# A fused LayerNorm, attention and gated-MLP kernel: the first stage's instructions, weight loads and buffer fills in another order

## The chip, the cores and the metric

One Trainium2 chip. The batch has eight sequences, and each of the eight cores runs the same program on one of them (2048 rows of 1024 numbers); the cores exchange nothing. The time is the device time of the slowest core in microseconds, median over runs.

## The reference

For each sequence `x` (float32, 2048 x 1024), with 16 heads of 64 and a hidden width of 3072:

```python
xn = (x - mean(x)) / sqrt(var(x) + 1e-5)
q, k, v = split(xn @ W_attn + b_attn)
att = q @ k.T / 8 / temperature + slope[h] * (j - i), masked to j <= i
y = (softmax(att) @ v) @ W_proj + b_proj
f = (silu(xn @ Wg.T) * (xn @ Wu.T)) @ Wd.T      # int weights / 127
out = x + y + f
```

## The kernel before, in words

The five engines run in-order programs written by hand, tied together by semaphores; nothing is scheduled by a compiler. There are three stages.

**First stage.** The sequence is cut into 16 tiles of 128 rows. For tile i: SyncE loads it (`xstage`, four buffers; load i waits for `v_xn` >= i-3, that is for tile i-4 to be normalised). VectorE takes statistics (two `bn_stats` L503, one `bn_aggr` L506). ScalarE takes the root of the variance (L641). VectorE takes its reciprocal (L510) and writes the normalised tile as bf16 (`xn_st`, L514). TensorE transposes it in eight matmuls with the identity (L745) into `ps_s` or `ps_gu` in turn, and ScalarE copies it into `xnT` (L648). `xnT` holds the whole sequence and is read by everything that follows. From it TensorE makes the values: a *value unit* is one row tile by one half (8 heads), eight matmuls of 512 columns into one of the two halves of `ps_t` (L770), copied to `Vt` by ScalarE (L656). The weights `wv_b` are loaded as two halves by GpSimd, whose DMAs also cast float32 to bf16 (L413). For each 512 rows, TensorE also makes q and k of the first pair of heads (*q/k unit*, two times eight matmuls, L710); VectorE copies q out (`evac_q`, L481), ScalarE copies k out (`evac_k`, L616). One matmul of one column (L752) turns the temperature into a vector, read back at L644.

The order before is one loop over tiles on each engine. TensorE's iteration i transposes tile i and then makes the values of tile i-1. ScalarE's iteration i takes the root of tile i, copies out transpose i-2 and then the values of that round. VectorE takes the statistics of tile i and then normalises tile i-1:

```python
for i in range(NT + 1):          # VectorE
    if i < NT: ...               # bn_stats x2, bn_aggr of tile i
    if i: ...                    # reciprocal, tensor_scalar of tile i-1
```

GpSimd, once x tiles 0 and 1 have landed, issues `wv_b` half 0, `wqk_b` of pair 0, `wv_b` half 1, and then fills rows 64 to 103 of `qx` and `kx` with twelve bf16 memsets (L421 to L425). Once tile 11 is normalised it issues the first two pairs of gate and up weights (`cast_gu(0)`, `cast_gu(1)`, L405 and L406), `wqk_b` of pair 1 and the output projection `wpj_b` (2 MB in bf16, L430).

**Second stage** (from L801 on in TensorE's program). `attention_plan` lists steps; each has score matmuls (L821), key-side matmuls (L802), value products (L837) and 512-column gate/up matmuls (L730) mixed in. `silu(f)` is GpSimd's part of gate/up unit f; its later weight loads are issued between those. **Third stage:** output projection plus down projection (L884, L889).

TensorE enters the second stage only behind the last q/k unit, when the last `evac_q`, `evac_k` and value copies are done. SyncE issues the shifts of q and k into `qx` and `kx` (L322) behind all its x loads.

## Time and profile before

| | |
|---|---|
| median of 3 runs | 1144.08 us (1143.51 to 1230.53) |
| the profiled execution | 1145.15 us |
| its span, first to last instruction of the slowest core (core 2) | 1143.6 us |
| spans of the eight cores | 1138.9 to 1143.6 us |
| TensorE matmul busy | 1084.3 us, 95% |
| VectorE, ScalarE, GpSimd busy | 628.9, 479.4, 267.1 us |

Times in the profile are counted from the span's start. An engine's idle time before an instruction is given with what ended it. A matmul's end is modelled, so rates are read from start to start.

### The profile page before, as it was taken

The numbers are of one execution on the slowest core, as the hardware profiler recorded it, in microseconds if no ns is written. First come the engines' busy times: TensorE is split into PE (matmuls) and PEld (weight loads), VectorE is DVE, ScalarE is ACT, GpSimd is POOL, SyncE is SP. The second block draws the span as 40 slices with busy tenths as digits, with TensorE's granted clock in tenths as the row PEclk, the third lists the DMA queues.
The fourth block names the chain that finished last, engine by engine and source line by source line (L and its number), as shares of the span: only waits on it lengthen the run. The fifth ranks groups of instructions, "written<-read, shape, count | busy, mean of one in ns | idle before, by whom it ended". The sixth has DMA issues, their size and how long they took to land.

```text
span 1143.6 us, 23885 instructions; the slowest of 8 cores (1138.9 to 1143.6 us)
## 1 busy us (share of the span) xinstructions
PE 1084.3 (95%) x7366; PEld 551.8 (48%) x7510; DVE 628.9 (55%) x1254; ACT 479.4 (42%) x869; POOL 267.1 (23%) x289
## 2 busy tenths in 40 slices
PE   3899899999999999999999999999999999999998
PEld 1344355555555545555555555555555344444443
DVE  5541867777776777677777777677873100000100
ACT  1443345655555555565565556555656200000000
POOL 7210121322222222132222112112223422222220
PEclk9999999999999999999999999999999999999999
DMA  8439023433413332153321213113521652525222
GB/s 185 132 93 176 19 53 75 79 71 71 89 34 66 78 83 63 42 88 67 68 59 34 62 42 62 34 31 73 168 61 38 217 189 74 184 74 184 74 74 74
DMA packets 57069, 98.34 MB, mean 86 GB/s; under 512 B 23292, under 2 KB 43909, under 8 KB 55862
## 3 DMA queue, kind: packets, MB, share of 16 engines
q0 software_dynamic: 7872, 35.66, 16.3%
q1 hardware_dynamic: 46178, 52.65, 15.6%
q10 hardware_dynamic: 2900, 8.51, 1.9%
q8 instruction: 68, 1.11, 0.4%
q14 instruction: 51, 0.42, 0.1%
HBM read 90.50 MB, written 27.26 MB: 103 GB/s over the span
## 4 chain that ended last, share of the span: by engine, by line
PE 86%; DVE 6%; issue 4%; DMA 2%; ACT 1%; POOL 1%; DVEq 0%; ACTq 0%; POOLq 0%; SPq 0%
PE ps_gu L730 24%; PE ps_dn L889 14%; PE ps_s L821 11%; PE ps_t L802 9%; PE ps_m L710 9%; PE ps_y L837 5%; PE ps_dn L884 5%; PE ps_t L770 5%; DVE cm L555 3%; DMA xstage<-xin 1%; PE ps_s L824 1%; PE ps_t L806 1%; DMA tile_s<-tiles 1%; DVE hst L491 1%; DVE nm L575 0%
## 5 line engine op out<-in xcount | busy, mean ns | idle before, releaser
L555 DVE TENSOR_REDUCE cm<-ps_s 128x1 f32<-128x512 f32 (+3 forms) x640 | 378.1, 607 | 144.6 <-PE ps_s L821 81.3
L672 ACT ACTIVATE pt<-ps_t 128x512 bf16<-128x512 f32 (+1 forms) x576 | 328.7, 575 | 297.8 <-PE ps_t L802 191.1
L730 PE MATMUL ps_gu<-xnT,wubuf 128*128 128x512 bf16 x720 | 246.1, 378 | 3.3 <-DVE hst L491 2.3
L730 PE MATMUL ps_gu<-xnT,wgbuf 128*128 128x512 bf16 x714 | 244.7, 378 | 2.4 <-ACT kst L616 1.2
L821 PE MATMUL ps_s<-kx,qx 67*128 67x512 bf16 (+3 forms) x640 | 213.7, 347 | 16.7 <-DVE cm L555 11.6
L802 PE MATMUL ps_t<-qx,kx 104*128 104x512 bf16 (+3 forms) x640 | 216.3, 348 | 1.5 <-DVE qx L585 0.8
L433 POOL TENSOR_SCALAR th_s<-th_s 128x512 f32<-128x512 f32 x96 | 59.4, 618 | 615.7 <-ACT th_s L624 615.7
L889 PE MATMUL ps_dn<-wdres,hb 128*128 128x512 bf16 x753 | 167.7, 379 | 0.8
L837 PEld LDWEIGHTS ps_y<-Vt,pt 128*128 128x128 bf16 x2176 | 125.3, 97 | 81.7 <-issue 0.2
L837 PE MATMUL ps_y<-Vt,pt 128*128 128x65 bf16 x2176 | 138.8, 193 | 0.5
L605 DVE SCALAR_TENSOR_TENSOR outsb<-ps_dn,xres 128x512 f32<-128x512 f32 x32 | 20.7, 686 | 205.1 <-PE ps_dn L889 205.1
L710 PE MATMUL ps_m<-xnT,wqk_b 128*128 128x512 bf16 x466 | 120.0, 378 | 0.7
L889 PEld LDWEIGHTS ps_dn<-wdres,hb 128*128 128x128 bf16 x768 | 75.1, 98 | 90.6
L439 POOL TENSOR_TENSOR gs_s<-th_s,gh_s 128x512 bf16<-128x512 f32 x96 | 111.0, 1156 | 26.4 <-POOL th_s L433 26.4
L821 PEld LDWEIGHTS ps_s<-kx,qx 67*128 67x128 bf16 x640 | 61.7, 96 | 102.9 <-issue 52.3
L730 PEld LDWEIGHTS ps_gu<-xnT,wubuf 128*128 128x128 bf16 x768 | 73.0, 98 | 57.0 <-issue 5.9
L730 PEld LDWEIGHTS ps_gu<-xnT,wgbuf 128*128 128x128 bf16 x768 | 73.5, 98 | 51.9 <-issue 1.9
L491 DVE SCALAR_TENSOR_TENSOR hst<-ps_gu,gs_s 128x512 bf16<-128x512 f32 x96 | 65.9, 686 | 39.3 <-POOL gs_s L439 32.5
L802 PEld LDWEIGHTS ps_t<-qx,kx 104*128 104x128 bf16 x640 | 63.3, 99 | 30.0 <-issue 4.0
L624 ACT ACTIVATE th_s<-ps_gu 128x512 f32<-128x512 f32 x96 | 57.1, 594 | 32.3 <-PE ps_gu L730 31.7
L770 PE MATMUL ps_t<-wv_b,xnT 128*128 128x512 bf16 x250 | 62.3, 403 | 4.7 <-DMA wv_b<-wv_r 2.7
L710 PEld LDWEIGHTS ps_m<-xnT,wqk_b 128*128 128x128 bf16 x480 | 41.9, 97 | 39.8 <-issue 0.4
(74 smaller groups left out, 737.1 us busy)
## 6 DMA issues: line engine op xcount, KB each, us to landing
h_sc<-hst SPq DMA_DIRECT2D x96, 128.0 KB, 1.9
hb<-h_sc SPq DMA_DIRECT2D x4, 3072.0 KB, 13.8
xstage<-xin SPq DMA_DIRECT2D x16, 512.0 KB, 6.8
xres<-xin POOLq DMA_DIRECT2D x16, 512.0 KB, 4.7
out<-outsb ACTq DMA_DIRECT2D x15, 512.0 KB, 2.7
wgbuf<-wg_r POOLq DMA_DIRECT2D x12, 512.0 KB, 5.7
wubuf<-wu_r POOLq DMA_DIRECT2D x12, 512.0 KB, 8.8
wd_sc<-wd_r POOLq DMA_DIRECT2D x12, 512.0 KB, 7.8
```

The lines of the kernel that those rows point to most:

```text
L433: e.tensor_scalar(th_s[f % 2][:, :], th_s[f % 2][:, :], 1.0, 1.0, AluOpType.add, AluOpType.mult).then_inc(sem["g_th"], 1)
L439: e.tensor_tensor(gs_s[f % 2][:, :], th_s[f % 2][:, :], gh_s[f % 2][:, :], AluOpType.mult).then_inc(sem["g_s"], 1)
L491: e.scalar_tensor_tensor(hst[f % 4][:, :], ps_gu[:, 512:1024], 1.0 / 127.0, gs_s[f % 2][:, :], AluOpType.mult, AluOpType.mult).then_inc(se ...
L555: e.tensor_reduce(cm[:, c0:c0 + 1], ps_s[:, s % 2 * 512:s % 2 * 512 + w], AX.X, AluOpType.max, negate=True).then_inc(sem["v_mx"], 1)
L672: e.activation(pt[t % NPT][:, 0:w], ps_t[:, t % 2 * 512:t % 2 * 512 + w], AF.Exp).then_inc(sem["a_e"], 1)
L710: mm = e.matmul(ps[:, :], wqk_b[p % 2][:, f0 + dc * 256:f0 + dc * 256 + 128], xnT[:, dc * T + tc * 512:dc * T + (tc + 1) * 512], start=(dc ...
L730: mm = e.matmul(ps_gu[:, r // 8 * 512:r // 8 * 512 + 512], w[:, w0:w0 + 128], xnT[:, dc * T + tb * 512:dc * T + tb * 512 + 512], start=(dc ...
L770: mm = e.matmul(ps_t[:, n % 2 * 512:n % 2 * 512 + 512], xnT[:, dc * T + tt * 128:dc * T + (tt + 1) * 128], wv_b[:, half * 4096 + dc * 512: ...
L802: mm = e.matmul(ps_t[:, c0 + off:c0 + off + w], k_[0:KT, kt * 128:(kt + 1) * 128], q_[0:KT, b * 512 + i0 * 128:(b + 1) * 512], start=(x == ...
L821: mm = e.matmul(ps_s[:, r0:r0 + w], q_[0:KS, b * 512 + i * 128:b * 512 + (i + 1) * 128], k_[0:KS, c0:c0 + w], start=True, stop=not diag)
L837: mm = e.matmul(ps_y[:, i * VW:(i + 1) * VW], pt[a % NPT][:, c0:c0 + 128], Vt[:, (kt * H + h) * VW:(kt * H + h + 1) * VW], start=(T0[n] == ...
L889: return e.matmul(ps_dn[:, r0:r0 + 512], hb[tb % 2][:, hc * 512 + ts * 128:hc * 512 + ts * 128 + 128], wdres[:, hc * 1024 + half * 512:hc ...
```

## The change

No arithmetic is changed except how constants are written into `qx` and `kx` (as 32-bit words, so half as many elements per fill). Everything else is order:

- VectorE: the code is split into `statistics(i)` and `normalise(i)`. Statistics of tiles 0 and 1 come first, then both are normalised; tile 2 as one; from tile 3 on `statistics(i + 1)` stands ahead of `normalise(i)`. `evac_q` 0, 1, 2 stand behind tiles 6, 8 and 13 (before: in iterations 6, 10 and 14).
- ScalarE: a first root on `eps_s` right at the start; then an order written out by hand: roots (`deviation`) of tiles 0 and 1, transposes 0 and 1, and so on. For tiles 4 to 7 the root stands behind the copy of the transpose before it. From tile 8 on, roots are three tiles and transposes two tiles ahead of the values of `for i`.
- TensorE: transposes 0 and 1, value units 0 and 1, transposes 2 and 3, then per tile 4 to 7 one value unit and one transpose; all values of tiles 0 to 7 in half 0 come before any of half 1; the second q/k unit before the first unit of half 1; then transposes two tiles ahead.
- GpSimd: `wv_b` half 0 in two pieces, issued when x tile 0 and x tile 1 have landed; `wqk_b` when the second piece has landed; half 1 when `wqk_b` has landed; six fills then, the other six behind tile 12; `cast_gu(1)` behind `silu(0)`, `wpj_b` behind `silu(6)`.
- SyncE: the load of x tile 3 waits for the first piece of `wv_b`.

```diff
 # SyncE
             for i in range(NT):
+                if i == 3:
+                    e.wait_ge(sem["l_wva"], 16)
...
 # GpSimd
+            e.dma_start(out=wv_b[:, 0:2048], in_=wv_r[0, :, 0:2048]).then_inc(sem["l_wva"], 16)
             e.wait_ge(sem["l_x1"], 16)
...
+            e.dma_start(out=wv_b[:, 2048:4096], in_=wv_r[0, :, 2048:4096]).then_inc(sem["l_wvb"], 16)
+            e.wait_ge(sem["l_wvb"], 16)
+            cast_qk(0)
+            e.wait_ge(sem["l_wq0"], 16)
+            e.dma_start(out=wv_b[:, 4096:6144], in_=wv_r[1, :, 0:2048]).then_inc(sem["l_wv1"], 16)
+            e.dma_start(out=wv_b[:, 6144:8192], in_=wv_r[1, :, 2048:4096]).then_inc(sem["l_wv1"], 16)
+            set_rows(0, 1)
             e.wait_ge(sem["v_xn"], NT - 4)
             cast_gu(0)
-            cast_gu(1)
             cast_qk(1)
-            e.dma_start(out=wpj_b[:, :], in_=wproj_r[:, :]).then_inc(sem["l_wp"], 16)
+            set_rows(1, 7)
...
             for f in range(NF):
                 silu(f)
+                if f == 0:
+                    cast_gu(1)
+                if f == 6:
+                    e.dma_start(out=wpj_b[:, :], in_=wproj_r[:, :]).then_inc(sem["l_wp"], 16)
...
 # VectorE
+            for i in range(3, NT):
+                if i + 1 < NT:
+                    statistics(i + 1)
+                normalise(i)
...
 # ScalarE
+            for i in range(4, 8):
+                deviation(i)
+                evac_v(i - 2, i - 1)
+                if i == 6:
+                    evac_k(0, 0)
+                evac_x(i)
...
+            for i in range(8, NT):
+                if i + 3 < NT:
+                    deviation(i + 3)
+                if i + 2 < NT:
+                    evac_x(i + 2)
+                evac_v(2 * i, 2 * i + 2)
+                if i == 12:
+                    evac_k(0, 2)
...
 # TensorE
+            transpose_x(0)
+            transpose_x(1)
+            values(0, 2)
+            transpose_x(2)
+            transpose_x(3)
...
+            for i in range(4, 8):
+                values(i - 2, i - 1)
+                if i == 6:
+                    first_qk(0)
+                transpose_x(i)
+            values(6, 8)
+            first_qk(1)
+            e.wait_ge(sem["l_wv1"], 32)
+            values(8, 11)
+            transpose_x(8)
+            values(11, 14)
+            transpose_x(9)
+            values(14, 16)
+            for i in range(8, NT):
+                if i + 2 < NT:
+                    transpose_x(i + 2)
+                values(2 * i, 2 * i + 2)
+                if i == 11 or i == 15:
+                    first_qk(i // 4)
```

TensorE's first rows before, to the second value unit (the transposes write `ps_s` and `ps_gu`, the value units `ps_t`):

```order
L745 MATMUL ps_s<-ident_s,xn_st 128x128 [waits l_id,v_xn]
L745 MATMUL ps_s<-ident_s,xn_st 128x128 x7
L745 MATMUL ps_gu<-ident_s,xn_st 128x128 [waits v_xn]
L745 MATMUL ps_gu<-ident_s,xn_st 128x128 x7
L770 MATMUL ps_t<-wv_b,xnT 128x512 [waits a_xe,l_wv0]
L770 MATMUL ps_t<-wv_b,xnT 128x512 x7
L745 MATMUL ps_s<-ident_s,xn_st 128x128 [waits v_xn,a_xe]
L745 MATMUL ps_s<-ident_s,xn_st 128x128 x7
L770 MATMUL ps_t<-wv_b,xnT 128x512 [waits a_xe]
```

The same rows of the changed kernel, to the transpose of tile 3:

```order
L807 MATMUL ps_s<-ident_s,xn_st 128x128 [waits l_id,v_xn]
L807 MATMUL ps_s<-ident_s,xn_st 128x128 x7
L807 MATMUL ps_gu<-ident_s,xn_st 128x128 [waits v_xn]
L807 MATMUL ps_gu<-ident_s,xn_st 128x128 x7
L823 MATMUL ps_t<-wv_b,xnT 128x512 [waits a_xe,l_wva]
L823 MATMUL ps_t<-wv_b,xnT 128x512 x3
L823 MATMUL ps_t<-wv_b,xnT 128x512 [waits l_wvb]
L823 MATMUL ps_t<-wv_b,xnT 128x512 x3
L823 MATMUL ps_t<-wv_b,xnT 128x512 [waits a_xe]
L823 MATMUL ps_t<-wv_b,xnT 128x512 x7
L807 MATMUL ps_s<-ident_s,xn_st 128x128 [waits v_xn,a_xe]
```

The first value unit now starts with a quarter of the weights and waits in its middle for the next quarter, and the second value unit has moved ahead of the transpose of tile 2.

VectorE around tile 3 before (`xstage` buffer 3 holds tile 3, buffer 0 then tile 4):

```order
L503 BN_STATS st_3<-xstage 128x6 [waits l_x3]
L503 BN_STATS st_3<-xstage 128x6
L506 BN_AGGR mv<-st_3 128x2 [waits v_ln]
L510 RECIPROCAL rs<-sd 128x1 [waits a_sd]
L514 TENSOR_SCALAR xn_st<-xstage,mv,rs 128x1024 [waits v_ln]
L503 BN_STATS st_0<-xstage 128x6 [waits l_x0]
```

In the rows before, the normalisation (L514) is that of tile 2. In the changed kernel:

```order
L515 BN_STATS st_3<-xstage 128x6 [waits l_x3]
L515 BN_STATS st_3<-xstage 128x6
L518 BN_AGGR mv<-st_3 128x2 [waits v_st]
L515 BN_STATS st_0<-xstage 128x6 [waits l_x0]
L515 BN_STATS st_0<-xstage 128x6
L518 BN_AGGR mv<-st_0 128x2 [waits v_st]
L523 RECIPROCAL rs<-sd 128x1 [waits a_sd]
L528 TENSOR_SCALAR xn_st<-xstage,mv,rs 128x1024 [waits v_rs,v_ag]
```

Tile 2 is normalised ahead of these rows; tile 3's normalisation stands behind the statistics of tile 4, as it did in the kernel before.

ScalarE around tiles 3 to 5 of the changed kernel (roots write `sd`, copies of transposes `xnT`, copies of values `Vt`):

```order
L674 ACTIVATE xnT<-ps_gu 128x8x128 [waits p_xT]
L699 ACTIVATE cvec_s<-ps_m 128x1 [waits p_c]
L669 ACTIVATE sd<-mv,eps_s 128x1 [waits v_ag]
L684 ACTIVATE Vt<-ps_t 128x8x64 [waits p_v]
L674 ACTIVATE xnT<-ps_s 128x8x128 [waits p_xT]
L669 ACTIVATE sd<-mv,eps_s 128x1 [waits v_ag]
```

Before, the root of a tile stood ahead of the copy of the transpose of two tiles earlier:

```order
L641 ACTIVATE sd<-mv,eps_s 128x1 [waits v_ln]
L648 ACTIVATE xnT<-ps_gu 128x8x128 [waits p_xT]
L656 ACTIVATE Vt<-ps_t 128x8x64 [waits p_v]
L641 ACTIVATE sd<-mv,eps_s 128x1 [waits v_ln]
L648 ACTIVATE xnT<-ps_s 128x8x128 [waits p_xT]
```

In the changed kernel the root of tile 4 is behind the copy of transpose 3, and that of tile 5 behind the copy of transpose 4.

## Rows read from the trace of the kernel before

**Rows 1.** The page: TensorE's busy time, and the last chain by engine.

```profile
PE 1084.3 (95%) x7366; PEld 551.8 (48%) x7510; DVE 628.9 (55%) x1254; ACT 479.4 (42%) x869; POOL 267.1 (23%) x289
...
PE 86%; DVE 6%; issue 4%; DMA 2%; ACT 1%; POOL 1%; DVEq 0%; ACTq 0%; POOLq 0%; SPq 0%
```

**Rows 2.** Busy time by stretch: length, engines, granted clock, DMA share, GB/s.

```profile
13.50:50.50 37.00, 25.10 (x120) 12.40 (x123) 20.26 (x37) 10.89 (x19) 20.88 (x11) 0.95 0.71 165
50.50:115.00 64.50, 58.96 (x324) 28.59 (x327) 20.49 (x42) 28.26 (x48) 3.28 (x6) 0.97 0.61 129
115.00:1143.60 1028.60, 1000.22 (x6924) 510.75 (x7060) 582.49 (x1164) 438.41 (x799) 236.79 (x262) 1.00 0.31 79
```

**Rows 3.** TensorE in order of time: start, length, what [idle before].

```profile
13.49 1.01 PE L745 MATMUL ps_s<-ident_s,xn_st 128*128 128x128 bf16 x8 [13.49 <-DVE xn_st L514]
21.40 3.57 PE L770 MATMUL ps_t<-wv_b,xnT 128*128 128x512 bf16 x8 [2.69 <-DMA wv_b<-wv_r]
...
28.33 0.61 PE L745 MATMUL ps_gu<-ident_s,xn_st 128*128 128x128 bf16 x8 [0.50 <-DVE xn_st L514]
...
36.37 0.94 PE L745 MATMUL ps_s<-ident_s,xn_st 128*128 128x128 bf16 x8 [3.79 <-DVE xn_st L514]
37.10 3.28 PE L770 MATMUL ps_t<-wv_b,xnT 128*128 128x512 bf16 x8
...
43.67 7.07 PE L770 MATMUL ps_t<-wv_b,xnT 128*128 128x512 bf16 x31
50.58 0.61 PE L745 MATMUL ps_gu<-ident_s,xn_st 128*128 128x128 bf16 x8
51.02 3.62 PE L770 MATMUL ps_t<-wv_b,xnT 128*128 128x512 bf16 x16
...
97.09 0.61 PE L745 MATMUL ps_s<-ident_s,xn_st 128*128 128x128 bf16 x8 [2.00 <-ACT xnT L648]
97.73 5.30 PE L770 MATMUL ps_t<-wv_b,xnT 128*128 128x512 bf16 x16
```

**Rows 4.** TensorE's first matmul of the second stage.

```profile
115.08 0.38 PE L730 MATMUL ps_gu<-xnT,wgbuf 128*128 128x512 bf16 x1 [1.25 <-ACT kst L616]
```

**Rows 5.** VectorE in order of time.

```profile
7.41 1.29 DVE L503 BATCH_NORM_STATS2 st<-xstage 128x6 f32<-128x512 f32 x2 [5.96 <-DMA xstage<-xin]
...
11.05 2.29 DVE L514 TENSOR_SCALAR xn_st<-xstage,mv,rs 128x1024 bf16<-128x1024 f32 x1
...
93.48 0.81 DVE L481 TENSOR_SCALAR qst<-ps_m,cvec_s,cbq_s 128x512 bf16<-128x512 f32 x1 [10.30 <-PE ps_m L710]
94.20 1.27 DVE L503 BATCH_NORM_STATS2 st<-xstage 128x6 f32<-128x512 f32 x2
...
95.71 0.14 DVE L510 RECIPROCAL rs<-sd 128x1 f32<-128x1 f32 x1
96.02 0.81 DVE L514 TENSOR_SCALAR xn_st<-xstage,mv,rs 128x1024 bf16<-128x1024 f32 x1 [0.18 <-DVE rs L510]
```

**Rows 6.** ScalarE and GpSimd in order of time.

```profile
51.64 0.28 ACT L641 ACTIVATE sd<-mv,eps_s 128x1 f32<-128x1 f32 x1
51.83 1.01 ACT L648 ACTIVATE xnT<-ps_gu 128x1024 bf16<-128x1024 f32 x1
...
11.00 1.80 POOL L421 MEMSET qx<- 32x2048 bf16 x1
```

**Rows 7.** DMA share and GB/s: x loads alone, weights alone, both.

```profile
4.00:8.00 4.00, 0.00 (x0) 0.00 (x0) 0.59 (x1) 0.00 (x0) 0.00 (x0) 1.00 0.96 237
12.00:14.00 2.00, 0.51 (x6) 0.54 (x7) 1.67 (x4) 0.00 (x0) 1.88 (x2) 1.00 0.75 110
16.00:20.00 4.00, 1.01 (x8) 0.78 (x8) 3.79 (x6) 1.66 (x3) 3.76 (x3) 1.00 0.98 154
```

**Rows 8.** Landing of DMAs, by line (`wpj_b`) and of all 16 x tiles.

```profile
wpj_b<-wproj_r POOLq DMA_DIRECT2D x1, 2048.0 KB, 31.2
...
DMA to landing us min/median/max: 3.4/6.8/14.5
```

More of the change, by code:

```diff
@@ L409, in _ @@
             e.memset(Vt.rearrange("p (g d) -> p g d", d=VW)[:, :, 64:65], 1.0).then_inc(sem["g_set"], 1)
             e.wait_ge(sem["l_x0"], 16)
+            e.dma_start(out=wv_b[:, 0:2048], in_=wv_r[0, :, 0:2048]).then_inc(sem["l_wva"], 16)
             e.wait_ge(sem["l_x1"], 16)
-            for half in range(2):
-                e.dma_start(out=wv_b[:, half * 4096:(half + 1) * 4096], in_=wv_r[half, :, :]).then_inc(
-                    sem[f"l_wv{half}"], 16)
-                if half == 0:
-                    cast_qk(0)
@@ new lines, in statistics, with normalise @@
+            def statistics(i):
+                b = i % 4
+                e.wait_ge(sem[f"l_x{b}"], 16 * (i // 4 + 1))
+                for k in range(2):
+                    e.bn_stats(st6[b][:, 6 * k:6 * k + 6], xstage[b][:, k * 512:(k + 1) * 512]).then_inc(
+                        sem["v_st"], 1)
+                e.wait_ge(sem["v_st"], 2 * i + 2)
+                e.bn_aggr(mv[b][:, :], st6[b][:, :]).then_inc(sem["v_ag"], 1)
+            def normalise(i):
+                b = i % 4
+                e.wait_ge(sem["a_sd"], i + 1)
+                e.reciprocal(rs[b][:, :], sd[b][:, :]).then_inc(sem["v_rs"], 1)
+                e.wait_ge(sem["v_rs"], i + 1)
+                e.wait_ge(sem["v_ag"], i + 1)
+                if i >= 4:
+                    e.wait_ge(sem["p_xT"], i - 3)
+                e.tensor_scalar(xn_st[b][:, :], xstage[b][:, :], mv[b][:, 0:1], rs[b][:, :],
+                                AluOpType.subtract, AluOpType.mult).then_inc(sem["v_xn"], 1)
```

196 lines of the change are left out of this document (101 added, 95 removed), and 2 rows, old and new, of the table SEMS.

## The prediction

> **What bounds the kernel now.** I read the page first: TensorE is busy 95% of the span and makes 86% of the chain that ended last [rows 1]. Then the busy times by stretch, to see where the rest is: from 115 us on it is busy 1000.2 of 1028.6 us, while between 13.5 and 50.5 us it is busy only 25.1 of 37.0 [rows 2]. So the second and third stages are dense, and what an order of the first stage can give lies ahead of 115 us. Then TensorE's own rows there. One value unit takes 1.73 us (four of them from 43.67 to 50.58), half a q/k unit is the same eight matmuls, a transpose of a tile 0.44 (50.58 to 51.02) [rows 3]. The whole first stage is 32 value units, 8 halves of q/k and 16 transposes: 55.4 + 13.8 + 7.0 = 76.2 us. It runs from 13.49 to 115.08 - 1.25 = 113.8 us [rows 3, 4], 100.3 us; 24 us of these are waits or matmuls at half rate, and another 13.5 pass before the first transpose. The waits that name a cause: 2.69 us for the values' weights, 3.79 for a normalised tile, 2.00 behind a q/k unit (97.09; the trace has a second one alike). At half rate the same matmuls take longer: 3.57 us for eight at 21.40, 3.28 at 37.10, and 5.30 for sixteen at 97.73, against 3.62 at 51.02 [rows 3]. The granted clock over those stretches is 0.95 and 0.97 of full speed [rows 2], so part of TensorE's time goes at its lower level, 1.2 GHz; the engine had sat idle 3.79 and 2.00 us just before two of these.
>
> The second stage does not begin before the last q and k are copied out: the 1.25 us at 115.08 [rows 4]. This dependence stays. So every microsecond by which the last q/k unit ends earlier goes into the total, as long as nothing of the second stage is late.
>
> **The change part by part.** I walk through the changed order with the durations above. Each time is an estimate from the rows named.
>
> *Start.* x tile 0 is used at 7.41 as before, and both statistics (1.5 us each) end at 10.4. The normalisation of tile 0 took 2.29 us, where the same form takes 0.81 at 96.02; it started at 11.05, and a fill on GpSimd ran from 11.00 for 1.80 us [rows 5, 6]. The fills now come after the weights, so it takes 0.81; ScalarE's first root, with the loading of its table, is made beforehand, which I put at 0.3 us of the way to 11.05. First transpose at 11.6 instead of 13.49. The copy out takes 1.0 [rows 6], so the first value unit may start at 13.9.
>
 The rows agree (0.55 us from a fill's end to the normalisation's end). By this rule the six fills that stay at 26 us and later can still hold VectorE.
>
> *The new fills.* No row has a fill with 32-bit words. Each costs a normalisation between nothing and 1.80 us, the row of a fill with 2048 elements [rows 6]; with 1024 elements I take half of that, 0.9. Six stand beside tiles 3 to 5, where the normalisation is on the path, but only one of them can hold each tile: 0 to 3 us in all. I take nothing, since VectorE mostly waits for data there, and keep 3 for the range.
>
> *Weights and x tiles.* x loads alone move 237 GB/s, casting weight loads alone 110, both together 154 [rows 7] (bytes as written). x tiles 0 to 2 are in by 9.5. The first piece of `wv_b`, 0.5 MB, then takes 3.4 to 4.8 us: landed near 14. The second, now beside x tile 3: near 18. x tile 3, issued at 14, lands near 19.5, and x tile 4 behind it, at 3.4 us per 0.5 MB, near 22.5.
>
> The Trainium skill, DMA: Bandwidth & Descriptors, section "Queues, rings and completion order", has each engine take turns between queues that have work. By that the wait put before x tile 3 only gives the weights the turns that the tile would have had. The tile is then later by what the piece takes, and that is in the times above; without it x tile 3 would be in by 11 to 12, and T3 below would hang on tile 4 alone.
>
> *Tiles 0 to 3.* Value units 0 and 1 end at about 22 (the first waits in its middle for the second piece; both at half rate, as at 21.40, since TensorE idled before). The transpose of tile 2 is queued behind them, at no cost: its tile is ready at 17. Tile 3's normalisation stands behind the statistics of tile 4: 22.5 + 1.5 + 1.1 (reciprocal start to end of normalisation, 95.71 to 96.83 [rows 5]) = 25.1. Transpose 3 at 25.3, where before it stood near 28.
>
> *Tiles 4 to 7.* Here ScalarE takes the root of tile i behind the copy of transpose i-1, so a ring closes: copy 1.0, root 0.2 (51.64 to 51.83), reciprocal and normalisation 1.1, transpose 0.44, and some 0.35 of handing over: 3.1 us a tile [rows 3, 5, 6]. TensorE has 2.2 us of work for it (one value unit and one transpose). Transpose 4 is at 28.9 (one value unit at half rate between), 5 at 32.0. Then value unit 4, the q/k unit and the transpose fill the ring: 6 at 37.7, 7 at 40.8. Here ScalarE's order costs about 0.9 us a tile, some 2.7 in all. The loads of `wqk_b` (landed near 26, used at 34) and half 1 of `wv_b` (near 36, used at 48) are hidden; if that cover were gone, the q/k unit would be late by the difference, which takes 8 us more of landing.
>
> *From there on.* After transpose 7: two value units and a q/k unit, to 48.1. Left are 24 value units, two q/k units, eight transposes: 41.5 + 6.9 + 3.5 = 51.9, to 100.0. One stall stays. `evac_q` 2 is ahead of statistics 15 and normalisation 14 on VectorE, the same chain as from 93.48 to 96.83 (3.35 us), while TensorE has only the k half, 1.73: with the handing over 1.8 us, near the 2.00 at 97.09 [rows 3, 5]. The other stall of this kind goes, because `evac_q` 1 is done long before transpose 10. Value copies, roots and x loads are ahead of TensorE: VectorE needs 2.6 us a tile against 3.9. That makes 101.8.
>
> *The clock.* Two stretches of half rate are likely to remain somewhere: behind the wait for transpose 3, and with an even chance behind the one stall at the end, 1.7 us each [rows 3]; one of the first kind is in the walk, so I add 1.7. The last q/k unit ends at 103.6 instead of 113.8: 10.2 us gained.
>
> *Second stage.* `cast_gu(1)` is needed only at unit 8, more than 80 us after its new place. `wpj_b` is read in the third stage only. It took 31.2 us to land [rows 8], now over weights of the second stage that are not due then. All cost nothing; the end of this cover is a rival.
>
> The sum, against the profiled execution: 1145.15 - 10.2 = 1135.0. The median of the runs is 1.1 below that execution, so 1144.08 - 10.2 = 1133.9 us.
>
> **The rivals.**
> *Late landing.* The second piece and x tile 4 come 3 us later than I took (weights at 110 GB/s throughout [rows 7]), and the ring of tiles 4 to 7 runs at half rate: a value unit and a transpose are then 4.3 us against 3.1, 3.6 in three tiles. For it: DMA is full there at 0.98. Against: what x tile 3 and the later weights had to share before is now held back. Time: 1133.9 + 6.6 = 1140.5.
> *Clean.* x tile 4 lands at 19.5 and no half rate beyond the first two value units: 3 + 1.7 off, 1129.2. For it: less in flight at once. Against: a tile took up to 14.5 us to land before [rows 8].
> *It does not pass on.* The second stage starts earlier but gives it back, its first steps being bound by shifts of q and k or by the weights of gate 0 that now stand closer: 1143. Against: they are issued some 14 us earlier as well, as tile 12 is.
> *Slower.* `wpj_b` stands in front of weights in GpSimd's queue: the next gate/up weights and a `wqk_b` are issued two units, some 20 us, behind it. It is one mechanism: a 31.2 us transfer ahead of a load that the pair's projections wait for. It makes the kernel slower from the point where the wait passes the 10.2 us gained; at 20 us, 1133.9 + 20 = 1154. Against: these weights are used a pair later, and no wait for weights is in the second stage before.
>
> **How the numbers follow.** Forecast 0.60, late landing 0.18, clean 0.12, not passed on 0.07, slower 0.03. The range takes in both landing cases: 1127.5 (clean, with the 1.7 of the last stall's clock off) to 1141. A change of 2% is 22.9 us, about what a measurement of this kernel can tell from none. Faster by that needs nearly all 24 us of waits and half rate gone: 0.02. Slower by that: 0.01. Within: 0.97.
>
> **What would show it.** First transpose at 11.6; transpose 3 at 25, its wait ended by VectorE; the ring of 3.1 us; the second q/k unit ending near 48; one stall of 1.8 behind the third q/k unit; the first gate matmul near 104.9; busy times from there on as before. The forecast is wrong if transpose 3 is before 22 or after 28, if waits on `a_v` or `wv_b` appear after 48, or if TensorE waits for DMA in the second stage.

## The result and the profile after

The changed kernel takes 1139.97 us (median of nine runs, the lowest 1139.73), the kernel before in the same series 1144.33 us. The ratio is 0.9967, with a 95% interval of 0.9958 to 0.9977: 4.4 us faster, where 10.2 were forecast. That is inside the stated range, but well short of the forecast gain. The profiled execution took 1140.19 us, its span 1138.6 us on core 2, the same core that the rows of before come from (span 1143.6 us), so the two traces can be laid side by side.

The page of the changed kernel, its engines and its last chain, against [rows 1]:

```profile
PE 1093.0 (96%) x7510; PEld 551.2 (48%) x7510; DVE 627.4 (55%) x1254; ACT 480.3 (42%) x870; POOL 257.3 (23%) x291
...
PE 88%; DVE 5%; issue 3%; DMA 2%; POOL 1%; ACT 1%; DVEq 0%; SPq 0%; POOLq 0%; ACTq 0%
```

The shares hardly move. (TensorE's count is higher because the trace of before lacks a few matmul records, not because work was added.) The difference stands in the rows of TensorE in order of time, changed kernel, to be read against [rows 3, 4]. Columns: start, length, what, [idle before].

```profile
12.27 1.01 PE L807 MATMUL ps_s<-ident_s,xn_st 128*128 128x128 bf16 x8 [12.27 <-DVE xn_st L528]
...
15.98 1.87 PE L823 MATMUL ps_t<-wv_b,xnT 128*128 128x512 bf16 x4 [1.64 <-DMA wv_b<-wv_r]
18.43 3.40 PE L823 MATMUL ps_t<-wv_b,xnT 128*128 128x512 bf16 x12 [0.58 <-DMA wv_b<-wv_r]
...
25.47 0.61 PE L807 MATMUL ps_gu<-ident_s,xn_st 128*128 128x128 bf16 x8 [3.19 <-DVE xn_st L528]
...
29.45 0.88 PE L807 MATMUL ps_s<-ident_s,xn_st 128*128 128x128 bf16 x8
...
33.77 0.61 PE L807 MATMUL ps_gu<-ident_s,xn_st 128*128 128x128 bf16 x8 [1.70 <-DVE xn_st L528]
...
43.01 0.61 PE L807 MATMUL ps_gu<-ident_s,xn_st 128*128 128x128 bf16 x8 [1.28 <-DVE xn_st L528]
...
50.36 5.34 PE L823 MATMUL ps_t<-wv_b,xnT 128*128 128x512 bf16 x24
...
86.73 0.61 PE L807 MATMUL ps_s<-ident_s,xn_st 128*128 128x128 bf16 x8 [2.44 <-DVE xn_st L528]
87.17 5.30 PE L823 MATMUL ps_t<-wv_b,xnT 128*128 128x512 bf16 x16
...
107.98 0.38 PE L794 MATMUL ps_gu<-xnT,wgbuf 128*128 128x512 bf16 x1 [1.25 <-ACT kst L644]
```

The reader is to see three things. The last q/k unit ends at 107.98 - 1.25 = 106.7, against 113.8 before: the first stage gave 7.1 us, not 10.2. The transposes of tiles 3 and 4 come where the walk of the prediction has them (25.47 and 29.45, forecast 25.3 and 28.9); from there on it is late: 33.77 for tile 5 (forecast 32.0), 43.01 for tile 7 (40.8), 50.36 for the end of the second q/k unit (48.1). And the one stall left, before the transpose of tile 14, takes 2.44 us and not 1.8; the sixteen matmuls behind it take 5.30 against 3.62 in [rows 3], the 1.7 of half rate that was counted. (The granted clock is 0.72 from 86 to 92 us.) That last part is not a fixed property of the kernel. The same place in the second trace of the same kernel, taken for the repeat below:

```profile
87.55 0.61 PE L807 MATMUL ps_s<-ident_s,xn_st 128*128 128x128 bf16 x8 [2.43 <-DVE xn_st L528]
87.99 3.62 PE L823 MATMUL ps_t<-wv_b,xnT 128*128 128x512 bf16 x16
```

The wait is as long, and no half rate follows (granted clock 1.00 from 86 to 92 us); the first stage ends at 105.9 there. The prediction gave this stretch an even chance.

But the total gained only 5.0 us from span to span (1143.6 - 1138.6). The second stage gave 2.1 of the 7.1 back. GpSimd multiplies the gate of every gate/up unit once, 96 times in the second stage, so its rows are a clock for how far the program has come. Kernel before, GpSimd in order of time:

```profile
121.59 1.16 POOL L439 TENSOR_TENSOR gs_s<-th_s,gh_s 128x512 bf16<-128x512 f32 x1 [0.21 <-POOL th_s L433]
...
429.04 1.16 POOL L439 TENSOR_TENSOR gs_s<-th_s,gh_s 128x512 bf16<-128x512 f32 x1 [0.27 <-POOL th_s L433]
...
913.27 1.16 POOL L439 TENSOR_TENSOR gs_s<-th_s,gh_s 128x512 bf16<-128x512 f32 x1 [0.27 <-POOL th_s L433]
```

The same three units (the first, the one numbered 34, the last) in the changed kernel:

```profile
114.49 1.15 POOL L448 TENSOR_TENSOR gs_s<-th_s,gh_s 128x512 bf16<-128x512 f32 x1 [0.21 <-POOL th_s L442]
...
423.51 1.16 POOL L448 TENSOR_TENSOR gs_s<-th_s,gh_s 128x512 bf16<-128x512 f32 x1 [0.27 <-POOL th_s L442]
...
908.28 1.16 POOL L448 TENSOR_TENSOR gs_s<-th_s,gh_s 128x512 bf16<-128x512 f32 x1 [0.27 <-POOL th_s L442]
```

The lead is 7.10 us, then 5.53, then 4.99. Taken unit by unit it does not melt away evenly: it drops by 0.37 at unit 12, 1.12 at unit 34, 0.36 at 55 and 0.36 at 77, and stays within 0.3 us of its level between.

What stands at these places is on VectorE. Changed kernel, VectorE in order of time, ahead of each drop:

```profile
221.06 0.17 DVE L603 CAST nm<-nmf 128x4 bf16<-128x4 f32 x1 [0.54 <-DVE nmf L594]
...
414.07 0.17 DVE L603 CAST nm<-nmf 128x4 bf16<-128x4 f32 x1 [0.52 <-DVE nmf L594]
414.34 0.99 DVE L605 TENSOR_TENSOR nm<-nmf,nm 128x4 bf16<-128x4 f32 x1
...
605.80 0.69 DVE L504 SCALAR_TENSOR_TENSOR hst<-ps_gu,gs_s 128x512 bf16<-128x512 f32 x1 [0.43 <-issue]
...
799.76 0.69 DVE L583 TENSOR_REDUCE cm<-ps_s 128x1 f32<-128x512 f32 x1 [0.29 <-issue]
```

And GpSimd and TensorE beside the second of them:

```profile
414.16 1.15 POOL L448 TENSOR_TENSOR gs_s<-th_s,gh_s 128x512 bf16<-128x512 f32 x1 [0.27 <-POOL th_s L442]
...
416.08 0.38 PE L910 MATMUL ps_s<-kx,qx 67*128 67x512 bf16 x1 [0.99 <-DVE cm L583]
```

The kernel before at the place of 414, VectorE:

```profile
420.36 0.20 DVE L575 CAST nm<-nmf 128x4 bf16<-128x4 f32 x1 [0.17 <-DVE nmf L566]
420.67 0.17 DVE L577 TENSOR_TENSOR nm<-nmf,nm 128x4 bf16<-128x4 f32 x1
```

Four times, about 193 us apart, VectorE begins its next instruction some 0.3 to 0.4 us later than anything it waits for explains; the kernel before has no idle time of this kind there. The changed kernel has more such pauses, at 337.61 and 529.69 us for example, which the lead does not feel. Four pauses of 0.35 are 1.4 us. At 414 the pause also brings the 4-element TENSOR_TENSOR under GpSimd's multiplication: it takes 0.99 instead of 0.17 and ends at 415.33, GpSimd's at 415.31, and the next scores wait 0.99 us. That is 0.8 more. Together 2.2 us, against a loss of 2.1.

The place of the pauses follows a count. Take the instructions that the trace records for VectorE in order, with the semaphore waits, which the timeline view leaves out. The first record behind each pause is then number 572, 956, 1212, 1596, 1852 and 2492: 60 and a multiple of 128 each time. There the record comes 0.39 to 0.44 us after the one before it; next to them a record that has nothing to wait for comes after 0.07. The kernel before has such pauses too, at the same counts, on other instructions. Number 60, for example, is this row of VectorE, and number 316 (at 154.76) comes after 0.42 us:

```profile
33.49 0.21 DVE L506 BATCH_NORM_AGGREGATE mv<-st 128x2 f32<-128x12 f32 x1 [0.51 <-DVE st L503]
```

The new order gives each of the 16 tiles one semaphore wait more on VectorE (`v_rs` and `v_ag` where `v_ln` was), 2864 records against 2848. So from the second stage on every pause falls 16 records earlier in the work, here onto instructions that TensorE waits for. The two readings of this, experiments 8 and 9 below, had to be told apart from a third, the later weights (experiment 7).

### The profile page after: what moved, and what is told of

It is laid out like the page before. It is cut to its first block, busy times and chain, and to the rows that moved or that the text cites. A ratio compares the mean times of both kernels' runs of the same rounds, so it can differ in the third digit from the quotient of the medians.

```text
span 1138.6 us, 24057 instructions; the slowest of 8 cores (1134.2 to 1138.6 us)
## 1 busy us (share of the span) xinstructions
PE 1093.0 (96%) x7510; PEld 551.2 (48%) x7510; DVE 627.4 (55%) x1254; ACT 480.3 (42%) x870; POOL 257.3 (23%) x291
## 3 DMA queue, kind: packets, MB, share of 16 engines
q8 instruction: 68, 1.11, 0.4%
## 4 chain that ended last, share of the span: by engine, by line
PE 88%; DVE 5%; issue 3%; DMA 2%; POOL 1%; ACT 1%; DVEq 0%; SPq 0%; POOLq 0%; ACTq 0%
PE ps_gu L794 26%; PE ps_dn L978 15%; PE ps_s L910 10%; PE ps_t L891 10%; PE ps_m L774 9%; PE ps_y L926 5%; PE ps_dn L973 5%; PE ps_t L823 5%; DVE cm L583 3%; PE ps_s L913 1%; PE ps_t L895 1%; DMA xstage<-xin 1%; DMA wv_b<-wv_r 1%; DVE hst L504 1%; DVE nm L603 0%
## 5 line engine op out<-in xcount | busy, mean ns | idle before, releaser
L794 PE MATMUL ps_gu<-xnT,wubuf 128*128 128x512 bf16 x768 | 261.8, 378 | 2.1 <-DVE hst L504 2.1
L794 PE MATMUL ps_gu<-xnT,wgbuf 128*128 128x512 bf16 x768 | 261.4, 378 | 1.2 <-ACT kst L644 1.2
L910 PE MATMUL ps_s<-kx,qx 67*128 67x512 bf16 (+3 forms) x640 | 213.6, 347 | 14.4 <-DVE cm L583 11.3
L774 PE MATMUL ps_m<-xnT,wqk_b 128*128 128x512 bf16 x480 | 122.4, 378 | 0.0
L652 ACT ACTIVATE th_s<-ps_gu 128x512 f32<-128x512 f32 x96 | 57.1, 594 | 32.9 <-PE ps_gu L794 32.3
```

Source lines behind the costliest of these rows:

```text
L774: mm = e.matmul(ps[:, :], wqk_b[p % 2][:, f0 + dc * 256:f0 + dc * 256 + 128], xnT[:, dc * T + tc * 512:dc * T + (tc + 1) * 512], start=(dc ...
L794: mm = e.matmul(ps_gu[:, r // 8 * 512:r // 8 * 512 + 512], w[:, w0:w0 + 128], xnT[:, dc * T + tb * 512:dc * T + tb * 512 + 512], start=(dc ...
L910: mm = e.matmul(ps_s[:, r0:r0 + w], q_[0:KS, b * 512 + i * 128:b * 512 + (i + 1) * 128], k_[0:KS, c0:c0 + w], start=True, stop=not diag)
```

## The experiments

The theory at this point: (A) the first stage is held by ScalarE's root behind each copy in tiles 4 to 7, and by the q copy ahead of normalisation 14 on VectorE; (B) the second stage loses 2 us by pauses of VectorE and its clash with GpSimd. The rivals: x tiles or weights land late (A'), and the later weight loads slow the second stage (B').

| run | median us | before us | ratio (95%) |
|---|---|---|---|
| 1 loads and fills alone | 1146.89 | 1144.76 | 1.0020 (1.0010 to 1.0029) |
| 2 no wait before x tile 3 | 1143.47 | 1144.76 | 0.9990 (0.9981 to 1.0000) |
| 3 roots ahead | 1139.74 | 1144.76 | 0.9957 (0.9944 to 0.9971) |
| 4 q copy 2 later | 1136.92 | 1144.76 | 0.9932 (0.9917 to 0.9947) |
| 5 all ahead | 1134.34 | 1144.48 | 0.9908 (0.9893 to 0.9924) |
| 6 fills early | 1139.32 | 1144.48 | 0.9959 (0.9946 to 0.9972) |
| 7 weights early | 1140.66 | 1144.48 | 0.9967 (0.9954 to 0.9979) |
| 8 narrow silu | 1134.24 | 1144.48 | 0.9914 (0.9900 to 0.9928) |
| 9 sixteen more on VectorE | 1139.68 | 1144.35 | 0.9961 (0.9949 to 0.9973) |
| 10 the best: 5, statistics 4 behind | 1133.07 | 1144.35 | 0.9899 (0.9884 to 0.9914) |
| 11 the best with the sixteen | 1134.88 | 1144.35 | 0.9914 (0.9902 to 0.9927) |
| the changed kernel again | 1140.03 | 1144.35 | 0.9963 (0.9950 to 0.9975) |

The last row repeats the changed kernel beside runs 9 to 11, on the record with this:

> The changed kernel itself, as the measure beside the three others. All theories: 1139.5 to 1140.5, ratio 0.996 to 0.997.

Its 1140.03 us lie 0.06 us from the first series' 1139.97. The intervals of the ratios are about 0.1% of the time to each side, so differences under about 1.5 us between runs are not shown by the medians. The ends of stages below are from one trace each.

**1. The new loads and fills under the old order of the engines.** The kernel before, with GpSimd's and SyncE's parts of the change:

```diff
@@ GpSimd @@
-            e.memset(Vt.rearrange...
+            e.wait_ge(sem["l_x0"], 16)
+            e.dma_start(out=wv_b[:, 0:2048], in_=wv_r[0, :, 0:2048]).then_inc(sem["l_wva"], 16)
+            e.wait_ge(sem["l_x1"], 16)
+            e.dma_start(out=wv_b[:, 2048:4096], in_=wv_r[0, :, 2048:4096]).then_inc(sem["l_wvb"], 16)
...
@@ SyncE @@
+                if i == 3:
+                    e.wait_ge(sem["l_wva"], 16)
```

> The kernel before with the change's GpSimd and SyncE parts alone (pieces of the value weights, x tile 3 behind the first piece, fills in 32-bit words and later, gate/up pair 1 and the projection weights later); the engines' own orders are the old ones. Theory (the loads and fills bring the start, the order the rest): first transpose near 12.3 us, first value unit near 16 instead of 21.4, but both stalls of 2.0 us behind the q/k units stay and half 1 of the value weights, which lands near 41, is waited for; first stage over at 110 to 112 (113.8 before, 106.7 changed), time 1141 to 1143. Rival (the order brings all, the loads nothing): first stage over at 113.5 or later, time 1144 or more. Rival (the loads bring nearly all of it): 107 to 108, 1140.

Measured: 0.2% slower than before, with the first stage over at 115.1; the theory's 110 to 112 was wrong. TensorE in order of time (core 6):

```profile
41.49 8.84 PE L785 MATMUL ps_t<-wv_b,xnT 128*128 128x512 bf16 x32 [6.51 <-DMA wv_b<-wv_r]
...
75.29 0.61 PE L758 MATMUL ps_s<-ident_s,xn_st 128*128 128x128 bf16 x8 [2.00 <-ACT xnT L661]
```

In the old order the second half of the values' weights is used at 35, and it now lands at 41.5: a wait of 6.51 us that the changed order, which needs them at 50, does not have. The stall of 2.00 at 75.29 stays, and a second one alike at 98.32. So the loads by themselves bring nothing. No run has the new order with the old loads, so what each adds to the other's gain is not separated.

**2. Without the wait before x tile 3.**

```diff
-                if i == 3:
-                    e.wait_ge(sem["l_wva"], 16)
```

> The changed kernel without the wait that puts x tile 3's load behind the first piece of weights. Theory (transpose 3 hangs on x tile 4, which stands behind tile 3 in the queue, so tile 3 itself in the gap gives 1 to 2 us): transpose 3 at 23.5 to 24.5 instead of 25.47, the value units' first piece later by 1 to 2, first stage over at 105.5 to 106.5, time 1139 to 1140. Rival (the wait protects the weights): value units 0 and 1 end 3 us later, transpose 3 at 26 or later, time 1141 or more.

```profile
17.30 1.87 PE L821 MATMUL ps_t<-wv_b,xnT 128*128 128x512 bf16 x4 [4.30 <-DMA wv_b<-wv_r]
21.70 4.52 PE L821 MATMUL ps_t<-wv_b,xnT 128*128 128x512 bf16 x12 [2.53 <-DMA wv_b<-wv_r]
```

(TensorE in order of time.) The two pieces of weights are used at 17.30 and 21.70, where the changed kernel has 15.98 and 18.43; the last q/k unit ends at 109.4, so the first stage ends 2.7 us later than there, and the span is 2.7 us longer (1141.3 us). That is too little by luck: this trace has no half rate behind the wait for tile 14, whose transpose is 4.4 us later than in the changed kernel's first trace. Against its second trace, which has none either, the first stage ends 3.6 us later, and the medians are 3.5 us apart. The wait guards the weights' landing, and is worth about 3.5 us; the rival of the expectation had it.

**3. Roots further ahead.** ScalarE takes root i+1 before the copy of tile i, through tiles 4 to 8:

```diff
             evac_x(2)
+            deviation(4)
             evac_x(3)
...
             for i in range(4, 8):
-                deviation(i)
                 evac_v(i - 2, i - 1)
                 if i == 6:
                     evac_k(0, 0)
+                deviation(i + 1)
                 evac_x(i)
             evac_v(6, 7)
-            deviation(8)
```

> The changed kernel with ScalarE's roots of tiles 4 to 8 ahead of the copy of the transpose before them. Theory (a ring of copy, root, normalisation and transpose sets the pace of tiles 4 to 7): the waits of TensorE before transposes 5 and 7 (1.70 and 1.28 us) go, the first stage is over at 103.5 to 104.5 instead of 106.7, time 1137 to 1138.5. Rival (x tiles or the fills set the pace there): the waits stay, 106 to 107, time 1140.

```profile
32.92 0.61 PE L807 MATMUL ps_gu<-ident_s,xn_st 128*128 128x128 bf16 x8 [0.29 <-DVE xn_st L528]
...
42.57 0.61 PE L807 MATMUL ps_gu<-ident_s,xn_st 128*128 128x128 bf16 x8 [1.68 <-DVE xn_st L528]
```

(TensorE.) The wait of tile 5 fell from 1.70 to 0.29, as theory A has it (its transpose is 0.85 us earlier; the rest of the fall is TensorE, which came to it later). That of tile 7 stayed, 1.68, and a row of VectorE of this run names what is late:

```profile
39.60 1.29 DVE L515 BATCH_NORM_STATS2 st<-xstage 128x6 f32<-128x512 f32 x2 [1.59 <-DMA xstage<-xin]
```

The q copy stands ahead of the statistics of tile 8 (39.60), and these wait for their tile, with the normalisation of tile 7 queued behind them: A' at one place. The first stage ends at 106.3, not at the 103.5 to 104.5 expected, and the span is 1138.2 us, 0.4 under the changed kernel's, which these runs cannot tell from nothing.

**4. The q copy 2 behind normalisation 14.**

```diff
-                if i == 13:
+                if i == 14:
                     evac_q(0, 2)
```

> The changed kernel with VectorE's copy of the third q unit behind the normalisation of tile 14 instead of 13. Theory (that copy holds up statistics 15 and normalisation 14): TensorE's wait of 2.44 us before transpose 14 goes, and with it the half rate of the 16 matmuls behind it (5.14 against 3.45 us); first stage over at 102.6 to 104.3, time 1136 to 1138. Rival (only the wait goes, the lower clock comes anyway): 104.3, 1137.7. Rival (transpose 14 then waits for something else): 106 to 107, 1140.

```profile
83.96 0.61 PE L807 MATMUL ps_s<-ident_s,xn_st 128*128 128x128 bf16 x8
84.40 3.62 PE L823 MATMUL ps_t<-wv_b,xnT 128*128 128x512 bf16 x16
...
103.53 0.38 PE L794 MATMUL ps_gu<-xnT,wgbuf 128*128 128x512 bf16 x1 [1.25 <-ACT kst L644]
```

(TensorE.) No idle time ahead of the transpose at 83.96, and the sixteen matmuls behind it take 3.62 instead of 5.30. The first stage ends at 102.3, 4.4 us earlier than in the changed kernel; the span is 1134.7, 3.9 us shorter, the median 3.1 us lower. One line's place was worth the 2.44 us of waiting, and 1.7 more in the executions where half rate follows it. Of the traces that wait 2.3 to 2.5 us there, six have the slow stretch (the changed kernel and experiments 3, 6, 7, 8 and 9), and two have not (the changed kernel again and experiment 2), so 4.4 us is the upper price and 3.1 us, the median's, the usual one.

**5. All of it.** Roots as in 3, but ahead of the k copy too, q copy 0 behind normalisation 7, q copy 2 behind 14:

```diff
-                if i == 6:
+                if i == 7:
                     evac_q(0, 0)
...
-                if i == 13:
+                if i == 14:
                     evac_q(0, 2)
...
                 evac_v(i - 2, i - 1)
+                deviation(i + 1)
                 if i == 6:
                     evac_k(0, 0)
```

> The changed kernel with three moves: ScalarE's roots of tiles 4 to 8 ahead of the copies (now also ahead of the copy of the first k unit), VectorE's copy of q unit 0 behind normalisation 7, that of q unit 2 behind normalisation 14. Theory (each wait goes by its own move, but transpose 7 then waits for x tile 8, whose statistics stand ahead of normalisation 7): transpose 7 at 41.5 to 42.5 instead of 43.01, no wait before transpose 14, first stage over at 101 to 102, time 1135 to 1136.5. Rival (the roots are worth nothing, x loads set the pace): 102.3 or more, 1136.9 as with the q copy alone.

```profile
32.22 0.61 PE L807 MATMUL ps_gu<-ident_s,xn_st 128*128 128x128 bf16 x8 [1.33 <-DVE xn_st L528]
...
100.73 0.38 PE L794 MATMUL ps_gu<-xnT,wgbuf 128*128 128x512 bf16 x1 [1.25 <-ACT kst L644]
```

(TensorE.) After tile 5, at 32.22, no transpose waits. The first stage ends at 99.5, 7.2 us before the changed kernel's, and the span is 7.2 us shorter too (1131.4), so a gain on top of the changed kernel passes on whole. In the medians it is 5.6 us. That is more than experiments 3 and 4 promise; which of the three moves brings the rest was not separated. Against the kernel before, its lead falls in the second stage from 14.4 to 12.2 us, the same 2.2 at the same four places of the program: what is lost there does not grow with what comes in.

**6. The fills early,** right behind the two weight pieces, as they stood ahead of the weights before:

```diff
             e.dma_start(out=wv_b[:, 2048:4096], ...
+            set_rows(0, 1)
+            set_rows(1, 7)
             e.wait_ge(sem["l_wvb"], 16)
```

> The changed kernel with all twelve fills back to the start, right behind the issue of the second piece of weights. They hold VectorE's normalisations of tiles 0 to 2 as before, and the weights of q and k are issued some 4 us later. Theory (the value weights land after the first transposes, so an early first transpose is worth nothing): first transpose later by 1 to 2 us, the first value unit still at 15.5 to 16.5, first stage over at 106.2 to 107.2, time 1139.5 to 1140.5. Rival (the forecast's: the start passes on): 108 to 109, 1142.

```profile
14.75 1.87 PE L823 MATMUL ps_t<-wv_b,xnT 128*128 128x512 bf16 x4 [0.87 <-DMA wv_b<-wv_r]
```

(TensorE.) The first transpose came at 11.43, 0.8 us earlier than in the changed kernel's trace and not later, as was expected. The value units still wait for their weights, so neither where the fills stand nor when the first transpose comes decides the start: transpose 3 is at 25.22, as in the changed kernel (25.47). But from there to the transpose of tile 5 it now takes 7.03 us (to 32.25) instead of 8.30: without fills beside it, the ring is 1.3 us shorter. (The other traces with ScalarE's order unchanged, the second one of the changed kernel and experiments 4, 7 and 8, have 7.70 to 8.82 for it.) The first stage ended at 105.2, the span is 1.1 us shorter (1137.5) and the median 0.65 lower, which the intervals leave open.

**7. The later weights early again** (gate/up 1 and the output projection behind tile 12):

```diff
             cast_gu(0)
+            cast_gu(1)
             cast_qk(1)
+            e.dma_start(out=wpj_b[:, :], ...
                 silu(f)
-                if f == 0:
-                    cast_gu(1)
-                if f == 6:
-                    e.dma_start(out=wpj_b[:, :], ...
```

> The changed kernel with the second pair of gate and up weights and the projection weights back behind tile 12. Theory (they are off the path at either place; the 2.1 us that the lead shrinks by in the second stage come from elsewhere): first stage over at 106.5 to 107.5, lead over the kernel before of 7 us at unit 0 and 5 at unit 95 of the gate/up units, time 1139.5 to 1141. Rival (the later projection weights cost the 2 us): lead stays 7, time 1138.

1140.66 us, and GpSimd's gate rows lead those of before by 6.75 us at the first unit and 4.19 at the last: the loss in the second stage is 2.6 us with the weights early, where the changed kernel's two traces lose 2.1 and 2.6. B' is wrong, and no cost or gain of the later weights shows.

**8. GpSimd's silu on 8 columns.** This kernel leaves out nearly all of silu and of its product, so its output is another.

```diff
-                e.tensor_scalar(th_s[f % 2][:, :], ...
+                e.tensor_scalar(th_s[f % 2][:, 0:8], ...
-                e.tensor_tensor(gs_s[f % 2][:, :], ...
+                e.tensor_tensor(gs_s[f % 2][:, 0:8], ...
+            e.memset(gs_s[0][:, :], 1.0)
+            e.memset(gs_s[1][:, :], 1.0)
```

> The changed kernel with GpSimd's two silu operations cut from 512 to 8 columns (it leaves out nearly all of silu and of its product, so the MLP's part of the output is another). Theory (VectorE's small operations on SBUF wait for GpSimd's instructions, and TensorE for VectorE then): no CAST of VectorE waits 0.5 us, the lead over the kernel before does not fall from 7 to 5 in the second stage, time 1135 to 1138. Rival (the lead is lost to something else): 1139.5 to 1140.5.

1134.24 us with a first stage that ends at 106.1, as in the changed kernel. The lead no longer falls at unit 34 by 1.12 but by 0.37, and stands at 7.5 us at unit 55 (5.3 in the changed kernel). The groups by line of this run, VectorE in the second stage (the last two numbers ahead of the idle time are busy us and mean ns):

```profile
L605 DVE CAST nm<-nmf 128x4 bf16<-128x4 f32 x48 | 8.5, 177 | 8.5 <-DVE nmf L596 8.4
```

and of the changed kernel:

```profile
L603 DVE CAST nm<-nmf 128x4 bf16<-128x4 f32 x48 | 11.9, 249 | 8.9 <-DVE nmf L594 8.8
```

The difference is 3.4 us of VectorE held by GpSimd in this one line. So the part of the loss beyond the pauses is GpSimd's. The pauses themselves stay, at the same counts: the two fills ahead of the first tile move them by two records, from the CAST at 221 and 414 to the reduction ahead of it (220.14 and 412.76), and they show at 257.56, 449.50 and 720.02 too. Past unit 55 the lead of this kernel rises to 12.0 at the last unit, so the narrow silu removes more waiting than the changed kernel had lost; 1134.24 us is not the price of the clash alone. (The traced execution was the slowest of the five, 1137.11 us: 3.9 of the 12.0 are gone again by its end, from a wait of 2.13 us at 901.95 and half rate behind it.)

**9. Sixteen small instructions more on VectorE,** ahead of the last q copy. If the pauses belong to a place in VectorE's program, they must move.

```diff
+            for j in range(16):
+                e.memset(pad_s[0:1, j:j + 1], 0.0)
             evac_q(0, NTB - 1)
```

> The changed kernel with sixteen one-element memsets on VectorE in its idle time ahead of the second stage, so that everything behind them stands sixteen instructions later in its program. Theory (VectorE pauses 0.35 us at fixed places of its own program; in the changed kernel two of them lie ahead of a CAST that TensorE waits for, and behind the second the next operation runs into a GpSimd one): no CAST comes 0.70 us after the row before it at the two places (221 and 414 us) of the changed kernel, the lead at gate/up unit 95 is 0.5 to 1.5 us more than 5.0 with the same first stage, time 1138.5 to 1139.5. Rival (the place in time or GpSimd alone decides): both CASTs stay late, 1140.

They moved, and the time did not change (1139.68). None stands at 221, 414, 606 or 800, and the only CAST that waits over 0.3 us for its reduction is at 828.19, where the lead does not move. They stand at 60 and a multiple of 128 as before, 16 records earlier in the work: the rows at 178.72, 371.22 and 828.19 are late by numbers 444, 1084 and 2620. VectorE's rows, where the largest drop now is (1.15 us, at unit 42):

```profile
486.57 1.16 DVE L586 TENSOR_REDUCE cm<-ps_s 128x1 f32<-128x384 f32 x2 [1.00 <-PE ps_s L916]
...
488.17 0.94 DVE L608 TENSOR_TENSOR nm<-cm,nm 128x4 bf16<-128x4 f32 x1
```

GpSimd and TensorE at the same place:

```profile
487.94 1.16 POOL L449 TENSOR_TENSOR gs_s<-th_s,gh_s 128x512 bf16<-128x512 f32 x1 [0.27 <-POOL th_s L443]
...
489.99 0.38 PE L894 MATMUL ps_t<-qx,kx 104*128 104x512 bf16 x1 [1.04 <-DVE qx L616]
```

VectorE has stood idle for 1.00 us ahead of the reduction at 486.57, which is number 1468; the kernel before has 0.63 there. 0.37 late, and the small TENSOR_TENSOR falls under GpSimd's again. The lead over before goes from 7.57 to 5.3 us, by drops of 0.17, 0.36, 0.25, 1.15 and 0.35: 2.3 us, as much as without the sixteen, at other places. My expectation of a gain was wrong, the theory of what the loss is made of holds.

**10. The best version.** Experiment 5, and the statistics of tile 4 behind the normalisation of tile 3:

```diff
             for i in range(3, NT):
-                if i + 1 < NT:
+                if i + 1 < NT and i > 3:
                     statistics(i + 1)
                 normalise(i)
+                if i == 3:
+                    statistics(4)
```

> The kernel of e5_all_ahead with the statistics of tile 4 behind the normalisation of tile 3. Theory (transpose 3 waits for the landing of x tile 4 and its statistics only because of that order): transpose 3 at 23.5 to 24.2 instead of 25.9, the first stage over some 1.5 to 2 us before e5's 99.5, time 1132.3 to 1133.5. Rival (the wait only moves to transpose 4, whose root is later now): 99.5, 1134.3.

```profile
24.09 0.61 PE L809 MATMUL ps_gu<-ident_s,xn_st 128*128 128x128 bf16 x8 [2.29 <-ACT xnT L676]
...
101.09 0.22 PE L912 MATMUL ps_s<-kx,qx 67*128 67x128 bf16 x1 [1.46 <-ACT kst L646]
```

(TensorE.) The transpose of tile 3 comes at 24.09 instead of 25.93 in experiment 5, but tile 5 is as late as there, and the first stage ends at 99.6, as there: the wait moved to the transpose of tile 4 (1.77 us at 28.60), as the rival has it. 1133.07 us is the lowest of all, 11.3 us under the kernel before; against experiment 5 the intervals overlap, so the last step is not shown to be worth anything.

**11. The best with the sixteen.**

> e10_stats4_behind with the sixteen memsets of e9_shift16. Theory: both gains add, 1131.3 to 1133. Rival (no gain by the shift): as e10_stats4_behind.

1134.88: no gain again. The transpose of tile 5 waited 3.01 us in its trace and the matmuls around it went at half rate, so its first stage ended at 102.5; the lead fell by 2.3 us in the second stage, as everywhere in this family.

## Why the prediction was right, and where it failed

**Right.** What bounds the kernel: everything gained came out of the first stage. Transpose 3 at 25.3 (25.47), its wait ended by VectorE, and transpose 4 at 28.9 (29.45); one stall of the second kind gone, one left, with 1.7 us of half rate behind it in one of two traces; the weights moved later at no cost that shows (experiment 7); no wait for weights after 48.

**Start, wrong without a price.** The first transpose was forecast at 11.6 and came at 12.27 (11.09 and 11.43 in other traces); the weights for the first value unit came at 15.98 and not 14. Neither moved the time, because the transpose of tile 3 was late anyway, as the walk had it: it hangs that transpose on x tile 4 and adds nothing for the earlier first one. That two errors of 0.7 and 2.1 us leave it within 0.2 us is in part luck, since the landing of x tile 4 was an estimate too.

**"The wait put before x tile 3 only gives the weights the turns that the tile would have had."** I gave this wait no price of its own. It is worth about 3.5 us (experiment 2). The Trainium skill, DMA: Bandwidth & Descriptors, section "Queues, rings and completion order", lets queues take turns; the run agrees, since with x tile 3 in flight beside them the two pieces come 1.3 and 3.3 us later.

**The ring of tiles 4 to 7, mis-sized.** Forecast 3.1 us a tile; the end of the second q/k unit came 2.3 us later. That is most of the 3.1 us that the first stage fell short. From tile 4 to 5 it took 4.3 us. VectorE's rows of the changed kernel show why:

```profile
31.74 0.16 DVE L523 RECIPROCAL rs<-sd 128x1 f32<-128x1 f32 x1 [1.48 <-ACT sd L669]
32.15 1.37 DVE L528 TENSOR_SCALAR xn_st<-xstage,mv,rs 128x1024 bf16<-128x1024 f32 x1 [0.24 <-DVE rs L523]
...
41.54 0.17 DVE L523 RECIPROCAL rs<-sd 128x1 f32<-128x1 f32 x1 [1.28 <-ACT sd L669]
```

and GpSimd's rows beside it:

```profile
32.02 0.95 POOL L421 MEMSET kx<- 8x1024 int32 x1
```

The root is late, as the ring has it (1.48 and 1.28 us), and a fill from 32.02 to 32.97 holds the normalisation of tile 5: 1.37 instead of 0.81, ending 0.55 us after the fill, like the one of before in [rows 5, 6]. I had put the six new fills at nothing, with 0 to 3 us as bounds. That was the term put at too little. Their length was forecast at 0.9 us and is mostly 0.94, and experiment 6 has their price at 1.3 us of the ring. What ScalarE's order costs shows in experiments 3 and 5: with the roots ahead the transpose of tile 5 comes at 32.9 and 32.2 instead of 33.8, and with the k and q copies moved as well tile 7 does not wait. Tile 5 still waits 1.33 us in experiment 5, no longer for its root, but behind the statistics of tile 6 and a normalisation of 1.39 us.

**The stall before tile 14, mis-sized.** 1.8 was forecast from a chain of 3.35 us. VectorE's rows of the changed kernel:

```profile
82.67 0.81 DVE L494 TENSOR_SCALAR qst<-ps_m,cvec_s,cbq_s 128x512 bf16<-128x512 f32 x1 [6.93 <-PE ps_m L774]
...
84.91 0.14 DVE L523 RECIPROCAL rs<-sd 128x1 f32<-128x1 f32 x1
85.66 0.81 DVE L528 TENSOR_SCALAR xn_st<-xstage,mv,rs 128x1024 bf16<-128x1024 f32 x1 [0.62 <-DVE rs L523]
```

From 82.67 to 86.47 it is 3.80 us; the normalisation begins 0.75 us after its reciprocal, where [rows 5] have 0.31. The 0.44 us more are one of VectorE's pauses: the record ahead of this normalisation is number 188, again 60 and a multiple of 128. The transpose waited 2.44. Experiment 4 takes the wait away, and with it the half rate that followed it in the first trace.

**"Second stage: every microsecond goes into the total."** This step failed. 7.1 us came in and 5.0 went out. The rival "it does not pass on" (0.07) was right that something is given back, but wrong in its mechanism: neither shifts of q and k nor gate weights are waited for. The loss is four 0.35 us pauses on VectorE and a clash with GpSimd of 0.8. Experiment 8 shows the clash, and experiment 9 that pauses and clash move together with VectorE's program. The pauses stand at the same counts of records in the kernel before, in the changed one and in experiments 8 and 9; what a changed program alters is the instructions that they fall on. The sum had no term for that: by the counts, the change's 16 semaphore waits more on VectorE, all in the first stage, shifted the pauses of the second. What VectorE does in the pauses was not found: the trace has no row for it. The page of the changed kernel lists two DMA queues of the kind `instruction` (68 packets, 1.11 MB, and 51 packets, 0.42 MB); whether the pauses have to do with them was not tested. Open, too, is the size of the loss: every kernel of the new order with the whole silu loses 2.1 to 2.6 us, with 2864 records on VectorE or with 2880, and experiment 1, with VectorE's program of before (2848), 0.6. A kernel of the new order with the 16 waits taken out again was not run.

The sum of the two failures in the first traces: 3.1 us in the first stage and 2.1 in the second, of 10.2. By the medians it is 5.8 in all. The prediction's remark that 2% is about what a measurement of this kernel can tell from none was too coarse: the interval of this ratio is 0.1% to each side.

## What to carry to other kernels

- A stall on TensorE can cost twice: its own length, and the matmuls that run at half rate behind it. Here 2.44 us of waiting, from the place of one copy in VectorE's order, were worth 4.4 us where the half rate came, and 3.1 us in the median; the same wait had none behind it in two of eight traces. Do not credit a change with the half rate from one trace. Look at each wait for the instruction that stands ahead of the awaited one on its engine, and ask who needs it sooner.
- Time gained in a stage is not time gained in the total, even when the next stage is dense and unchanged. Lay a repeating row of the later stage (here GpSimd's 96 multiplications) of both traces side by side: it shows where a lead is lost to within one unit. And count the records of the engine that pauses: a few waits added in one stage can move a loss in the next.
- Before crediting a step with an earlier start, name what the next step waits for. The earlier first transpose was worth nothing, since the weights bound; the wait that holds back a tile was worth about 3.5 us, since it let them land.
